# Reordering three steps of the first attention stage: a weight tile's comparison on VectorE, an output copy on ScalarE, transposes on TensorE

## What is computed

```python
x = x + _L0_attn_ref(_layernorm(x), Wq, Wkv_down, Wk_up, Wv_up, Wo)   # 8 heads of 64, 1024 tokens
x = x + _L0_ffn_ref(_layernorm(x), w1, w2, h1, h2, w3)                # ternary weights, scaled
x = x + _L1_attn_ref(_layernorm(x), wq, wk, wv, wo)                   # 16 heads of 16, rotary
x = x + _L1_ffn_ref(_layernorm(x), w_gate, w_up, w_down)              # int weights / 127
```

```python
q = (x @ Wq.T).reshape(b, t, 8, 64)
kv_latent = x @ Wkv_down.T
k = (kv_latent @ Wk_up.T).reshape(b, t, 8, 64)
v = (kv_latent @ Wv_up.T).reshape(b, t, 8, 64)
attn = jax.nn.softmax(einsum('bqhd,bkhd->bhqk', q, k) * 64 ** -0.5, axis=-1)
out = einsum('bhqk,bkhd->bqhd', attn, v).reshape(b, t, 512) @ Wo.T
```

## Time and profile before

| what | value |
|---|---|
| median of 3 runs | 2413.9 us (2413.8 to 2413.95) |
| the profiled execution | 2416.73 us |
| its span | 2415.0 us |
| busy: PE, DVE, ACT, POOL | 2335.1 (97%), 1512.1 (63%), 1344.8 (56%), 1045.6 us (43%) |
| granted clock of PE, mean | 0.992 of full speed |
| turns of the first attention | 43.1 to 776.2 us in the trace |

### The profile page before, as it was taken

How to read it: one execution, slowest core, us unless ns; L and a number is a source line. 1 busy time by engine, 2 the same in 40 slices (tenths; PEclk the granted TensorE clock), 3 DMA queues, 4 the chain that set the end, 5 groups by cost and what they waited for, 6 DMA issues and landing times. The chain is left out here.

```text
span 2415.0 us, 39030 instructions
## 1 busy us (share of the span) xinstructions
PE 2335.1 (97%) x15265; PEld 1450.2 (60%) x15265; DVE 1512.1 (63%) x1934; ACT 1344.8 (56%) x1787; POOL 1045.6 (43%) x674
## 2 busy tenths in 40 slices
PE   6989999999999999999999999999999999999899
PEld 4545555555555788888888887444444444443588
DVE  6877777787784224312322223779989889998364
ACT  3555555554444444444444443478778778778643
POOL 1656776766677346556556556030000000000354
PEclk8999999999999999999999999999999999999999
DMA  1221321321212445555555556434333323332132
GB/s 45 77 69 54 97 77 57 97 68 56 66 49 69 148 166 181 176 193 183 175 192 186 175 195 190 122 89 85 85 76 74 91 70 72 92 84 47 60 119 82
DMA packets 156836, 259.04 MB, mean 107 GB/s; under 512 B 37004, under 2 KB 97292, under 8 KB 156300
## 3 DMA queue, kind: packets, MB, share of 16 engines
q1 hardware_dynamic: 156652, 256.53, 35.6%
HBM read 206.52 MB, written 60.68 MB: 111 GB/s over the span
## 5 line engine op out<-in xcount | busy, mean ns | idle before, releaser
L1839 DVE TENSOR_REDUCE m_mraw<-m_R 128x2 f32<-128x1024 f32 x512 | 622.7, 1221 | 71.7 <-PE m_R L129 60.6
L1690 ACT ACTIVATE m_P<-m_R 128x1024 f32<-128x1024 f32 x512 | 523.6, 1025 | 152.1 <-PE m_R L129 151.9
L584 ACT ACTIVATE a_P<-a_S 128x1024 f32<-128x1024 f32 x256 | 248.7, 1023 | 215.2 <-PE a_S L129 214.2
L129 PE MATMUL m_O<-m_P,m_V 128*17 128x256 f32 x4096 | 330.7, 395 | 4.4 <-ACT m_P L1690 2.5
L882 POOL TENSOR_TENSOR a_accp<-a_accp,a_P 128x1024 f32<-128x1024 f32 x96 | 251.6, 2621 | 15.2 <-ACT a_P L584 6.0
L1944 POOL TENSOR_TENSOR m_act0l<-m_xf,m_act0h 128x512 fp32r<-128x512 f32 x128 | 164.8, 1290 | 212.3 <-ACT m_xf L1752 112.9
L129 PE MATMUL a_O<-a_P,a_V 128*64 128x512 f32 x1024 | 247.7, 605 | 4.4 <-ACT a_ON L592 4.4
L129 PE MATMUL m_R<-m_act0h,wt 128*128 128x512 f32 x640 | 251.4, 393 | 0.2 <-DMA wt<-wcopy 0.2
L129 PE MATMUL m_R<-m_act0l,wt 128*128 128x512 f32 x640 | 250.4, 391 | 0.0
L715 DVE TENSOR_REDUCE a_mraw<-a_X 128x2 f32<-128x1024 f32 x164 | 199.8, 1218 | 78.6 <-PE a_X L129 78.6
L129 PE MATMUL m_R<-m_Q,m_K 64*128 64x512 f32 x800 | 200.6, 498 | 2.5 <-DVE m_mraw L1839 2.2
(11 more groups left out here) (246 smaller groups left out, 4232.7 us busy)
## 6 DMA issues: line engine op xcount, KB each, us to landing
wt<-wcopy SPq DMA_DIRECT2D x176, 512.0 KB, 3.4
m_K<-bounce_k SPq DMA_DIRECT2D x96, 128.0 KB, 5.4
m_ln_x<-x SPq DMA_DIRECT2D x23, 512.0 KB, 4.2
a_tile<-in_L_ffn_tiles SPq DMA_DIRECT2D x22, 512.0 KB, 4.5
wcopy<-in_L_ffn_tiles SPq DMA_DIRECT2D x22, 512.0 KB, 5.2
x<-xres SPq DMA_DIRECT2D x78, 128.0 KB, 3.1
m_Q<-bounce_q SPq DMA_DIRECT2D x150, 64.0 KB, 2.2
xres<-x SPq DMA_DIRECT2D x64, 128.0 KB, 2.7
```

Source lines behind the costliest of these rows:

```text
L129: return pe.eng.matmul(out, lhsT, rhs, start=start, stop=stop, skip_group_check=True)
L584: act.eng.activation(P[n % NP][:, :, :], psS[n % 2][:, :, :], ACT.Exp, scale=SCALE).then_inc(s_exp)
L1690: act.eng.activation(P[h % 4][:, :, :], pair(key)[:, :, :], ACT.Exp, scale=SCALE).then_inc(R.free(key))
L1839: dve.eng.tensor_reduce(mraw[u % 2][:, at, :], pair(key)[:, :, :], AX.X, ALU.max).then_inc(R.free(key))
```

## The change

It moves three calls, each on one engine; nothing is added or taken away.

1. ACT: `keep_out(u - 1)` stands in front of `tile_high` (it stood behind).
2. DVE: `tile_low`, the weight tile's step, stands behind `reduce` of the second maximum and `residual` (it stood in front of both).
3. PE: of the two weighings of a turn, the first stands in front of the transposes `turn_pe`, the second behind (both stood behind). In turns without transposes nothing changes on PE.

```diff
@@ -665,10 +665,10 @@
                 if norm_at(u, j) and norm_at(u, j)[1] >= 5:
                     half = norm_at(u, j)[1] - 5
                     norm.scale_act(act, norm_at(u, j)[0], 4 * half, 4 * half + 4)
+                if j == 0 and u:
+                    keep_out(u - 1)
                 if tile_at(u, j) and tile_at(u, j)[1] == "round":
                     tile_high(tile_at(u, j)[0])
-                if j == 0 and u:
-                    keep_out(u - 1)
@@ -817,12 +817,12 @@
                 if m:
                     for n in (2 * m - 2, 2 * m - 1):
                         add(n)
-                if tile_at(u, j):
-                    tile_low(*tile_at(u, j))
                 if ahead < STEPS:
                     reduce(ahead + 1)
                 if pending:
                     residual(*pending)
+                if tile_at(u, j):
+                    tile_low(*tile_at(u, j))
@@ -1063,12 +1063,13 @@
                     values(values_at(u, j))
                 if rows_at(u, j):
                     max_rows(rows_at(u, j))
+                if m:
+                    weigh(2 * m - 2)
                 if turn_at(u, j):
                     for f in range(2):
                         norm.turn_pe(pe, turn_at(u, j)[0], f, turn_at(u, j)[1], ident[:, :])
                 if m:
-                    for n in (2 * m - 2, 2 * m - 1):
-                        weigh(n)
+                    weigh(2 * m - 1)
```

## The result

**Slower.** The changed kernel takes 2435.51 us (median of 5 runs, 2428.01 to 2439.71), the kernel before 2413.95 in the same session (5 runs, 2413.8 to 2420.24). The ratio is 1.0077, with a 95% interval from 1.0064 to 1.009, so the change costs 15 to 22 us. The forecast was 2418, in a range from 2400 to 2427: the sign and the main mechanism were those of its sum (no change and slower had stood equal, at 0.39 each), the size was not, and the time lies above the range.

The account below looks back on a forecast made before the run. The prediction took PE, busy 97% of the span, as the bound, so only its idle time counted. Its terms 18.8 - 4.1 - 3.2 - 7.5 gave +4.0 us on 2413.9, so 2418, range 2400 to 2427.

Parts of the forecast that it names:

- What bounds the kernel: Whole kernel: PE is busy 97% of the span, so only its idle time counts; at most some 28 us winnable.
- The comparison in j = 1: First attention: the moved comparison asks 0.6 us after POOL's L879 begins, ends late, and PE waits anew: +18.8 us.
- units 1 to 4: Comparisons of the early units: nothing in 1 and 2, +0.8 and +0.9 us in 3 and 4.
- rival B: Comparison gets the SBUF operands first, so L879 waits and not PE: faster, 2397 to 2407.5, taken as 2400; chance 0.20.
- The output copy: Units 5, 13 and 21: passing the rounding and the comparison's move shorten PE's waits, 2.2, 0.95 and 0.95: -4.1 us.
- The transposes: Turns (5, 2), (5, 3), (13, 3), (21, 3): a weighing fills PE's wait for the bank, 0.8 each: -3.2 us.
- rival C: Late exponentials or late inverse use up their cover and POOL falls back: slower by more, 2427 us; chance 0.15.
- The five-step tiles: Turns 91 to 115: twelve waits of 11.9 us leave 1.6, two new ones add 2.8: -7.5 us.
- The two new waits: Five-step tiles, where PE did not wait: 0.9 us at (24, 1), a cast, and 1.9 at (27, 1), a comparison.
- The sum: First attention: 18.8 - 4.1 - 3.2 - 7.5 = +4.0 us, uncertainty about 5; forecast A, chance 0.60, own range 2412 to 2424.

Follow-up runs that it names:

- the second execution: The unaltered changed kernel run and profiled once more, against the kernel before: 2436.81 us, ratio 1.0085; profiled span 2441.6 us.
- POOL held: Full change plus POOL's L879 waiting for the comparison, against the kernel before: 2403.98 us, ratio 0.9952; the same without PE's move: 2402.14 us, ratio 0.9946.
- the wait that takes the lock away: Full change plus POOL's L882 of step 6 waiting for DVE's last addition L741, against the kernel before: 2423.92 us, ratio 1.0037.
- three other kernels: Against the kernel before: ACT's move alone, 2414.54 us; PE's move alone, 2420.43 us; extra DVE reductions put in to make PE wait, 2456.32 us.
- the two waits: Full change plus POOL's L879 waiting for the comparison and L882 for DVE's addition L741, against the kernel before: 2397.99 us, ratio 0.993.
- the kernel with waits put in: Kernel before plus four spare DVE reductions in front of the first reduction of turns (8, 2) to (20, 2): 2456.32 us, ratio 1.0169.

## Why the prediction was wrong

**What bounds the kernel:** right that only PE's idle time counts, and most of it lay in the turns named; the latent turns were not named, and what the waits do to PE's clock was left out. Both are below.

**The comparison in j = 1** (forecast +18.8): right in mechanism and close in size, +20.8. L879 3.51 us into the turn (forecast 3.5), the end 1.08 behind POOL's end, L766 about 2.8 us, PE's wait 0.95 (forecast 1.2). What was mis-sized inside it is units 1 to 4, +4.4 where +1.7 was put; the placing gave 0 in unit 2, and (2, 2) grew by 1.5 us while (2, 1) shrank by 1.1. The prediction speaks of L879 alone, and in units 1 to 4 the comparison met L882. That the +16.4 of units 6 to 22 lies so near its 17.1 is in part luck: in the second execution (7, 1) and (10, 1) fell the other way, and they are +22.4, of which 3.4 is clock. The experiment that only exchanges the order of the two requests takes more than these 20.8 us away (22.8 in the profile), so the cause is shown, and rival B, in which the comparison goes first, is what that kernel does: B's sum was 2397 to 2407, and it measured 2404.

**The output copy** (-4.1): -3.9, right in the change as a whole. The sentence "Passing the rounding takes 1.04 off" failed as a cause: alone, the ACT move gains nothing, since the comparison waits for the rounding that was passed. The gain is of both moves together.

**The transposes** (-3.2): -3.1 in their own turns, and **the first step that failed**. "A weighing of 0.86 us" that "now fills that" was carried to the end of the turn and no further. The 0.8 us that (5, 2) and (5, 3) each gain are taken from the time in which the inverses' DMA was hidden, POOL's L882 so falls in front of L741, and PE loses 4.7 us of waiting in (6, 0), (14, 0), (22, 0), 6.4 with the clock. In the profiles of PE's move alone and of the whole change beside the kernel without it, the net of this step is a loss of 3 to 4 us. The runs bear this out only weakly (1.001, from 0.9998 to 1.0022, alone; overlapping intervals with the other two moves; nothing with POOL held). That the latent turns are its price is shown by the turns of all these kernels and by the wait that takes the lock away. The prediction had warned of the very thing for POOL (rival C, "the late inverse") but looked for it where PE's waits grow, not where they shrink.

**The five-step tiles** (-7.5): -8.3, with some luck. About 1.9 of it, in (25, 2), is a lost lock of the one execution of before that three other kernels with the same code don't have; the sum had counted that wait as sure. The two new waits came behind the steps forecast, those of (24, 1) and (27, 1): (24, 2) is 0.9 longer and (27, 2) 1.7.

**The sum** (+4.0): **the second failed step is that it knows one clock.** It adds up waits and gives each its length. The waits of some 2 us that the change makes are followed by stretches at 1.2 GHz, 1.7 us each: one in the profiled execution, five in the second one. With the mean clock at 0.9896 to 0.9884 instead of 0.9917, that is 5 to 7 us on the median. The trace of before could have bounded it: it has stretches at half clock at the start (29.6 to 46.7 us) and after the stage (3.4 us at 783.9), and none between, so the price of a stretch could be read and only its number not. It also has a warning against any simple count: (5, 1), where PE waits 1.61 and 1.21 us, is followed by none. The terms as measured, 20.8 - 3.9 - 3.1 + 6.4 - 8.3 = +11.9, of which 1.7 is clock, leave +10.2 for waits. The second profile has 5.0 us more of waits, so these are 10 to 15 us, which agrees with the 13 to 15 at full clock; with the clock's 5 to 7 that is the measured 15 to 22. The 5 us of waits between two profiles of one kernel are the three meetings that fell differently. For (10, 1) the way of the inverses differs: L870 begins 2.14 us into (10, 0) in the first profile and 0.52 in the second. What shifts the requests of the other two is left open.

**Rival C** had the size (2427) by another mechanism: in the units 8 to 12 and 15 to 20 L870, which needs the inverses, begins 0.5 to 1.4 us into the turn (u, 0), before and after, with one exception after, (10, 0) at 2.1; in (7, 0) it is 2.3 in both. It isn't what happened.

**The skill's rule.** The Trainium skill, "SBUF — State Buffer", Who interferes with whom, says that of DVE and GpSimd the first to ask has the shared port and the other is fully held up; the comparison in its old, its new and its exchanged order agrees with it: 1.08 behind POOL's end where POOL asked first, 1.22 us long and POOL later where DVE did. The Trainium skill, "Perfetto Trace Analysis", GPSIMD Engine Instruction, calls GpSimd's spans in a profile unreliable, and was the reason why a lead of 0.6 us was not taken as proof; here it could have been: 0.56 us of lead in the profile decided as the rule says, and so did 0.13 and even 0.01.

## What to carry to other kernels

Where DVE and POOL both work from SBUF, ask for each pair which request comes first, and whether the short operation with someone behind it can be made the first: a wait on the engine that nobody waits for cost nothing here and was worth more than every reordering (the two waits turned +0.8% into -0.7%). When a change takes a wait away, follow the next thing whose time is set by a DMA and not by the turn, since it now comes later against everything else. And weigh a wait of 2 us on TensorE in an otherwise full stretch at more than its length, by a chance that one profile doesn't show: it was followed by half clock in three of thirteen cases in one kernel, and in one or five places in two profiles of another. So take a second profile before an account in microseconds is believed.

## What the runs showed of the hardware

A DVE operation of two SBUF operands of 128 x 1024 that meets a running POOL operation ends 1.08 us behind the latter's end: the comparison (243.82 + 2.36 to 247.26) and the addition (183.36 + 2.39 = 185.75 to 186.84) show the same figure, though one asks 0.56 and the other 0.13 behind POOL's start. It takes 1.22 alone, so being late by 0.01 us costs as much as 2.25 (3.47 in (7, 1) of the second profile). Where DVE asks first, POOL is held up in turn: L879 took 3.45 instead of 2.38. A cast from integers (L763), 0.68 alone, took 2.92 in (25, 2) of the kernel before, where POOL's L882 asked 0.02 ahead.

TensorE's granted clock fell to half (0.51 to 0.54, 1.2 GHz) for 3.4 us in 23 places inside the first attentions of the profiled kernels. In each PE had just waited 1.6 to 2.9 us, at once or in two waits close together. It was not so after every such wait: three of thirteen in the kernel with waits put in, none after the 2.8 us of (5, 1) in the kernel before, and one and five places in two profiles of the same kernel. The Trainium skill, "TensorE: Matmul & The Clock Gate", A second HAM failure mode, tells of a kernel whose short idle times between groups of matmuls make the clock swing between its two levels; these traces agree in kind, with single waits of 2 us in an otherwise full stretch. What is to be seen of the scatter between runs follows it: the profiled executions of the change had a mean clock of 0.991 at a span of 2426.2 and 0.988 at 2441.6.
